# A table-lookup MLP on one core: first-layer sums split into two banks by chunk parity, with the next half transposed ahead of a half's product

## The reference

```
emb = tables[t][cat[t]]                      # 26 tables, 512 x 128 each
linear = sum over t of emb[t] + relu(numerical @ w_wide + b_wide)
x = relu(concat(numerical, emb[0], ..., emb[25]) @ W1 + b1)     # 3341 -> 256
x = relu(x @ W2 + b2)                                           # 256 -> 128
y = sigmoid(x @ W3 + b3 + linear)                               # 512 x 128
```

## Time and profile before

| | |
|---|---|
| median of 3 runs | 248.84 us (247.8 to 249.22) |
| the profiled execution's own time | 247.35 us |
| its span, first to last instruction | 245.5 us |
| PE busy | 110.2 us (45%) |
| POOL busy | 95.0 us (39%) |
| DVE busy | 37.7 us (15%) |
| ACT busy | 21.0 us (9%) |
| mean granted PE clock | 0.791 |

### The profile page before, as it was taken

One profiled execution on the slowest core, in us unless ns is written; L12 is line 12 of the kernel. 1 busy time (PEld: TensorE's weight loads), 2 busy tenths in 40 slices (PEclk: granted clock), 3 DMA queues, 4 the chain that ended last, 5 costly groups with the idle time before them and its releaser, 6 DMA issues.

```text
span 245.5 us, 2014 instructions
## 1 busy us (share of the span) xinstructions
PE 110.2 (45%) x398; PEld 67.5 (28%) x398; DVE 37.7 (15%) x106; ACT 21.0 (9%) x45; POOL 95.0 (39%) x108
## 2 busy tenths in 40 slices
PE   2657004500700004500009059979799991007795
PEld 0143001300300001300004026545466660005594
DVE  2031001000100002000001023244244430001132
ACT  0100000000000000000000001011011120001242
POOL 5777777777777777777750000000000000000000
PEclk9999999955695555875555759999999997555999
DMA  6994315444443353433231012131000000000001
GB/s 189 297 234 100 58 50 89 62 51 50 103 56 51 58 46 95 57 50 54 54 54 43 0 47 72 62 87 52 8 3 4 4 1 3 1 2 0 0 13 32
DMA packets 11163, 14.05 MB, mean 57 GB/s; under 512 B 3196, under 2 KB 8031, under 8 KB 11151
## 3 DMA queue, kind: packets, MB, share of 16 engines
q0 software_dynamic: 3168, 6.49, 17.7%
q10 hardware_dynamic: 3359, 3.63, 5.1%
q1 hardware_dynamic: 4624, 3.80, 5.1%
HBM read 13.65 MB, written 0.26 MB: 57 GB/s over the span
## 4 chain that ended last, share of the span: by engine, by line
SPq 54%; issue 35%; PE 8%; DMA 1%; ACT 1%; DVE 1%; ACTq 0%; DVEq 0%
SPq L229 48%; SPq L224 6%; PE first_layer L335 2%; PE first_layer L378 2%; PE mlp L401 1%; DMA first_cat<-in_r_cat_features 1%; ACT emb_t L559 1%; PE turn L320 1%; DMA emb<-in_L_rec_tables 0%; PE total L409 0%; PE turn L369 0%; PE total L395 0%; PE first_layer L351 0%; PE total L390 0%; ACT late_t L572 0%
## 5 line engine op out<-in xcount | busy, mean ns | idle before, releaser
L335 PE MATMUL first_layer<-emb_t,w 128*128 128x512 f32 (+3 forms) x104 | 58.2, 692 | 104.2 <-issue 90.3
L270 POOL DMA_INDIRECT emb<-in_L_rec_tables,row_idx x98 | 92.5, 944 | 30.0 <-issue 29.5
L335 PEld LDWEIGHTS first_layer<-emb_t,w 128*128 128x128 f32 x104 | 21.9, 231 | 124.4 <-issue 106.2
L500 DVE TENSOR_TENSOR emb_sum<-turn,emb_sum 128x512 f32<-128x512 f32 (+3 forms) x25 | 16.0, 638 | 182.0 <-issue 106.4
L559 ACT COPY emb_t<-turn 128x512 f32<-128x512 f32 (+3 forms) x26 | 14.1, 544 | 207.5 <-PE turn L320 75.8
L320 PE MATMUL turn<-ident,emb 128*128 128x128 f32 x94 | 17.6, 314 | 20.7 <-DMA emb<-in_L_rec_tables 18.1
L344 PE MATMUL total<-hot,block_rows 128*128 128x256 f32 (+1 forms) x98 | 25.0, 386 | 0.0
L320 PEld LDWEIGHTS turn<-ident,emb 128*128 128x128 f32 x94 | 14.3, 166 | 36.1 <-issue 35.8
L344 PEld LDWEIGHTS total<-hot,block_rows 128*128 128x128 f32 (+1 forms) x98 | 17.8, 199 | 1.6
L486 DVE TENSOR_SCALAR hot<-pick_row,row_no 128x256 f32<-128x256 f32 x49 | 14.8, 352 | 0.0
L378 PE MATMUL first_layer<-late_t,w 128*128 128x128 f32 x32 | 5.4, 291 | 0.6 <-ACT late_t L572 0.4
(11 more groups left out here) (51 smaller groups left out, 28.9 us busy)
## 6 DMA issues: line engine op xcount, KB each, us to landing
emb<-in_L_rec_tables SPq DMA_DIRECT2D x256, 0.5 KB
block_rows<-in_L_rec_tables ACTq DMA_DIRECT2D x12, 256.0 KB, 2.8
w<-in_L_rec_W SPq DMA_DIRECT2D x2, 1152.0 KB
emb<-in_L_rec_tables ACTq DMA_DIRECT2D x128, 0.5 KB
emb<-in_L_rec_tables,row_idx POOLq DMA_INDIRECT x98
w<-in_L_rec_W SPq DMA_DIRECT2D x1, 768.0 KB, 5.2
w<-in_L_rec_W SPq DMA_DIRECT2D x1, 256.0 KB
out<-y SPq DMA_DIRECT2D x4, 64.0 KB, 1.6
```

Source lines behind the costliest of these rows:

```text
L270: nc.gpsimd.indirect_dma_start(emb[:, t, c, :], None, rows, bass.IndirectOffsetOnAxis(ap=index, axis=0)).then_inc(landed, 16)
L335: mm = nc.tensor.matmul(first_layer[k][:, cols], w1[:, t, chunk(k)], emb_t[:, i % SLOTS, cols], start=False, stop=False, skip_group_check= ...
L500: nc.vector.tensor_tensor(emb_sum[:, cols], turn[i % 2][:, cols], emb_sum[:, cols], ALU.add).then_inc(added, 1)
```

## The change

The 512 columns of the first layer are held as two halves: half 0 is chunks 0 and 2, half 1 is chunks 1 and 3. Each has a bank of 256 used columns for each half of the hidden units (four banks in place of two, and the two banks `mlp` are gone; the second layer writes into free columns of the banks `first_layer[0][q]`). PARTS is now 47 half tables in place of 26 mostly whole ones, so every part has two tiles. Tile (0, 2) moves into an earlier part together with (0, 0), and (0, 1) and (0, 3) make part 44. Behind it stand only the two halves of table 25.

PE now transposes part i+1 before it multiplies part i. `emb_t` has 6 slots of 256 columns in place of 4 of 512. ACT issues 4 row fetches after each copy in place of 8. The late tables are 23 and 24. Their transposed tiles are added into `emb_sum` by DVE (`add_tile`), so that one product (`begin_total`) brings the sum into `total`. The picked tiles are chunks 1 and 3 of table 12, and their product stands right after part 40. The order of the tail is written anew. SP's program, the number of gathers (99), of row fetches (384), of pieces (13) and of one-hot blocks (49) stay as they are.

```diff
-LATE = 2
-HALVED = 2
-SLOTS = 4
+LATE_TABLES = (23, 24)
+SLOTS = 6
-ROWS_A_STEP = 8
-PICK_TABLE = 22
-PICK_FROM = 2
+ROWS_A_STEP = 4
+PICK_TABLE = 12
+PICK_HALF = 1
...
+    OTHERS = [t for t in range(1, T) if t not in LATE_TABLES]
+    PARTS = [(t, q) for t in OTHERS[:-4] for q in range(2)] + [(0, 0)]
+    PARTS += [(t, q) for t in OTHERS[-4:-1] for q in range(2)] + [(0, 1)]
+    PARTS += [(t, q) for t in OTHERS[-1:] for q in range(2)]
+    PARTS.remove((PICK_TABLE, PICK_HALF))
+    PICK_PARTS = (2, LAST - 8)
+    PICK_END = LAST - 7
+    def tiles(i):
+        t, q = PARTS[i]
+        return [(t, q + 2 * j) for j in range(HALF)]
...
+        def late_turn(n):
+            return turn[(LAST + n) % 2][:, 0:P]
+        def first_half(k, q):
+            return first_layer[k][q][:, 0:HW]
+        def first_chunk(k, c):
+            return first_layer[k][c % 2][:, chunk(c // 2)]
+        def second_chunk(c):
+            return first_layer[0][c % 2][:, HW + c // 2 * P:HW + (c // 2 + 1) * P]
...
+            turn_part(0)
             for i in range(LAST):
-                turn_part(i)
+                if i + 1 < LAST:
+                    turn_part(i + 1)
                 for j in blocks(i):
                     pick_block(j)
-                sum_part(i)
+                if i + 1 < LAST:
+                    sum_part(i)
                 if i == PICK_END:
                     sum_picked()
...
             def sum_tile(n):
                 c, g = divmod(n, LATE)
                 pe.wait_ge(late_copied, n + 1)
-                for k, (done, ready) in enumerate([(h1_low_done, h1_low_ready), (h1_high_done, h1_high_ready)]):
-                    if c >= 1 and g == 0:
-                        pe.wait_ge(ready, c)
+                if c >= 2:
+                    pe.wait_ge(h2_ready, c - 1)
...
             for c in range(CH):
                 n = c * LATE
                 turn_tile(n)
-                if c >= 1:
-                    add_late(c - 1)
+                if c == 0:
+                    sum_part(LAST - 1)
+                else:
+                    sum_tile(n - 1)
+                    begin_total(c - 1)
+                if c >= 2:
+                    layer3(c - 2)
+                turn_tile(n + 1)
+                sum_tile(n)
+                if 1 <= c < CH - 1:
                     layer2(c - 1)
-                sum_tile(n)
-                turn_tile(n + 1)
-                begin_total(c)
-                if c >= 1:
-                    layer3(c - 1)
-                sum_tile(n + 1)
-            add_late(CH - 1)
+            sum_tile(TILES - 1)
+            layer2(CH - 2)
             layer2(CH - 1)
+            layer3(CH - 2)
+            begin_total(CH - 1)
             layer3(CH - 1)
...
+            def add_tile(n):
+                c, g = divmod(n, LATE)
+                dve.wait_ge(late_copied, n + 1)
+                if n == 0:
+                    dve.wait_ge(added, LAST)
+                else:
+                    dve.wait_ge(late_added, n)
+                nc.vector.tensor_tensor(sum_chunk(c), late_turn(n), sum_chunk(c), ALU.add).then_inc(late_added, 1)
             for c in range(CH):
-                sum_late(c)
-                relu_h1_high(c)
-                relu_h2(c)
+                add_tile(c * LATE)
+                if c >= 1:
+                    relu_h1_high(c - 1)
+                add_tile(c * LATE + 1)
+                if 1 <= c < CH - 1:
+                    relu_h2(c - 1)
+            relu_h1_high(CH - 1)
+            relu_h2(CH - 2)
+            relu_h2(CH - 1)
...
             for c in range(CH):
                 copy_tile(c * LATE)
+                if c >= 1:
+                    relu_h1_low(c - 1)
+                if c >= 2:
+                    squash(c - 2)
                 copy_tile(c * LATE + 1)
-                if c >= 1:
-                    squash(c - 1)
-                relu_h1_low(c)
+            relu_h1_low(CH - 1)
+            squash(CH - 2)
             squash(CH - 1)
```

More of the change, by code:

```diff
@@ L66, in rows_apart @@
         return (t, c) in BY_SYNC + BY_SCALAR
-    BODY_TILES = [(0, 0)] + [(t, c) for t, lo, hi in PARTS for c in range(lo, hi) if (t, c) != (0, 0) and not rows_apart(t, c)]
+    BODY_TILES = [(0, 0)] + [tile for i in range(LAST) for tile in tiles(i) if tile != (0, 0) and not rows_apart(*tile)]
     def part_of(t, c):
-        return next(i for i, (u, lo, hi) in enumerate(PARTS) if u == t and lo <= c < hi)
+        return PARTS.index((t, c % 2))
     def by_pool(i):
-        t, lo, hi = PARTS[i]
-        return sum(not rows_apart(t, c) for c in range(lo, hi))
+        return sum(not rows_apart(t, c) for t, c in tiles(i))
     rows = tables.rearrange("t v d -> (t v) d")
@@ L282, in _ @@
                 c, g = divmod(n, LATE)
-                gather(BODY + g, c, column(BODY + g, c), late_gathered[n])
+                gather(LATE_TABLES[g], c, column(LATE_TABLES[g], c), late_gathered[n])
         @block.tensor
@@ L299, in _ @@
             pe.wait_ge(w1_num_loaded, 16)
-            for k in range(KH):
-                nc.tensor.matmul(first_layer[k][:, :], w1_num[:, chunk(k)], num_t[0:NUM, :], start=True, stop=True)
+            for q in range(2):
+                cols = num_t[0:NUM, :].rearrange("n (j q p) -> n q j p", j=HALF, q=2)[:, q, :, :]
+                for k in range(KH):
+                    nc.tensor.matmul(first_half(k, q), w1_num[:, chunk(k)], cols, start=True, stop=True)
             pe.wait_ge(small_loaded, 16 * SMALL)
@@ L316, in turn_part @@
                     pe.wait_ge(added, i - 1)
-                for c in range(lo, hi):
+                for j, (t, c) in enumerate(tiles(i)):
                     if (t, c) in fetched:
                         pe.wait_ge(fetched[t, c], 16 * P)
-                    mm = nc.tensor.transpose(turn[i % 2][:, chunk(c)], emb[:, t, c, :], ident[:, :])
+                    mm = nc.tensor.transpose(turn[i % 2][:, chunk(j)], emb[:, t, c, :], ident[:, :])
                 mm.then_inc(turned, 1)
@@ L383, in begin_total @@
             def begin_total(c):
-                if c == 0:
-                    pe.wait_ge(added, LAST)
-                    pe.wait_ge(pick_added, 1)
+                pe.wait_ge(late_added, (c + 1) * LATE)
                 if c >= 2:
                     pe.wait_ge(y_ready, c - 1)
[L390 to L396, removed]
+                nc.tensor.matmul(total_of(c), sum_chunk(c), ident[:, :], start=True, stop=False, skip_group_check=True)
             def layer2(c):
@@ L544, in _ @@
             act.dma_start(w2[:, :, :], W2.rearrange("(k p) n -> p k n", p=P)).then_inc(small_loaded, 16)
-            act.dma_start(pick_cat[:, :], cat[PICK_TABLE, PC:B].partition_broadcast(P)).then_inc(pick_cat_loaded, 16)
+            for j in range(HALF):
+                c = PICK_HALF + 2 * j
+                act.dma_start(pick_cat[:, chunk(j)], cat[PICK_TABLE, chunk(c)].partition_broadcast(P)
+                              ).then_inc(pick_cat_loaded, 16)
             act.wait_ge(ident_steps, 2)
@@ L553, in _ @@
             regs = []
-            for i, (_, lo, hi) in enumerate(PARTS):
-                cols = slice(lo * P, hi * P)
+            for i in range(LAST):
                 act.wait_ge(turned, i + 1)
@@ L571, in copy_tile @@
                 act.wait_ge(late_turned, n + 1)
-                nc.scalar.copy(late_t[:, n, :], turn[n % 2][:, 0:P]).then_inc(late_copied, 1)
+                nc.scalar.copy(late_t[:, n, :], late_turn(n)).then_inc(late_copied, 1)
             def relu_h1_low(c):
                 act.wait_ge(h1_low_done, c + 1)
-                nc.scalar.activation(h1[:, 0, chunk(c)], first_layer[0][:, chunk(c)], ACT.Relu,
+                nc.scalar.activation(h1[:, 0, chunk(c)], first_chunk(0, c), ACT.Relu,
                                      bias=b1_col[:, 0:1]).then_inc(h1_low_ready, 1)
```

91 lines of the change are left out of this document (39 added, 52 removed).

## The result

The changed kernel takes 241.48 us (median of 4 runs, 240.63 to 241.65) against 248.47 us before; the ratio is 0.971, 95% interval 0.9683 to 0.9737. Forecast were 243.5 us and a range of 237.5 to 250.

What follows compares the result with a forecast made beforehand. SP's row fetches were taken to bound the kernel. Gains of 4.1 us behind the landing and 1.3 us in the tail took 247.35 to 241.95 us; with the median 1.5 us above, 243.5 us was forecast, range 237.5 to 250.

Steps and rivals of the forecast that it cites:

- What bounds the kernel: Whole kernel: SP's row fetches end at 221.7 us, plus 21.5 us of work behind, plus 2.3 us for sigmoid and store.
- SP's chain at zero: SP's row fetches: program and 99 gathers unchanged, so cost zero, with 4 us either way as uncertainty.
- first two rivals: SP's slow stretch gets shorter or quicker, 231 to 240 us (chance 0.14), or longer, 245 to 254 us (chance 0.19).
- The rule of the Trainium skill: Slow stretch: SP's slowness would hang on how many trace records the core makes; 231 to 240 or 245 to 254 us.
- The body under cover: Half parts ahead of the landing: end at 206 to 216 us, 6 to 16 us of cover, cost zero.
- Behind the landing: From tile (0, 3)'s landing to the second late tile's transpose: 6.3 us, no gaps for copies, 4.1 us gained.
- Tail: Work from the second late tile's transpose on: 9.1 us against 10.43 before, 1.3 us gained.
- Sum: Whole kernel: 5.4 us less, 241.95 us for the profiled execution; median 1.5 us above that, 243.5 us.

## Why the prediction was right, and where it was off

**What bounds the kernel.** Right: SP's last row sets the start of the end. With SP's second tile given to POOL, and product 43 ahead of part 44, the time falls by 15.6 us on the same chip. How much of that is the product's place isn't separated; behind a landing it was worth 0.9 to 1.9 us.

**SP's chain at zero.** Right to 0.8 us: the last row landed at 222.6 and not 221.8 us, which is no more than it varies between executions. Neither of the first two rivals came about: the stretch ended at 143.03 against 143.01 us, with 8 table pieces in it by then and not 6, and half as many rows to a copy. The slowness is there in one lot and not in another, and ACT is held up beside POOL's gathers also without any row fetch. The rule of the Trainium skill weighed there ("NOTIFIC — the notification-queue block", section 7.1: inside, the block that takes down the records holds its producers back and loses none) is neither shown nor excluded by that, since no run here shows the block.

**The body under cover.** Right: 8 half parts by 143 us (6 to 9 were said), the end at 206.8 us (206 to 216), 15.8 us of cover (6 to 16). That transposing ahead would save as much as 12.6 us here was not said; it costs and gains nothing until the cover goes.

**Behind the landing.** The order and the missing gaps were right. The term was 6.3 us to the second late tile and measured 5.9. The clock was back within the second product and not behind it. When it returns is not the kernel's alone: the same kernel on another chip needed 6.65 us for this. So that the term came out within 0.4 us is in part luck.

**Tail.** This term was mis-sized by the most: 9.1 us forecast, 8.34 measured. I counted the second layer at 0.55 to 0.61 us; 0.55 is its distance to the next group in the earlier trace rows (236.40 to 236.95), and in the new order that distance is 0.45 (230.47 to 230.92 in the changed kernel). That is 0.1 to 0.15 us for each chunk. I had rounded the other steps up by about 0.1 each, and the sum takes the last product to its end while the 10.43 us beside it goes to its start, which is 0.2 more. The two passes saved for each chunk are 0.89 us of the 2.09 gained; the other 1.20 are there also in the run that sums the late tiles as before (9.23 against 10.43), so they come from the rest of the new tail. Which of its waits gives how much isn't shown.

**Sum.** The profiled execution was forecast at 241.95 us and took 241.46. It is this close because misses offset each other: 0.8 us lost at the landing, 0.4 and 0.8 gained behind it. The median was forecast 1.5 us above it, since the kernel before had been so in three runs; after the change the two agree (241.46 and 241.48). That offset lies within what executions differ by and was not to be added, and it is most of the 2.0 us between forecast and median. The gain in medians, 7.0 us, is 1.2 above that in spans for the same reason.

**What stays open.** What the slow stretch is, and why it ends so long after the last gather. It was seen in lots where the kernel before takes 248 us, holds SP, ACT and with it PE, leaves POOL's cadence alone, and ends 16.0 to 16.8 us after POOL's last gather starts. No two lots of the experiments had the same chip, so whether it belongs to the chip or to something else that differs between lots isn't told. And the changed kernel itself was not timed on a chip without it: its variants with one more gather gained 2.6 to 2.7% there. That this is the shorter tail, behind the last gather, is likely and not shown.

## What to carry to other kernels

Find the transfer whose landing starts the end of the kernel, and price an edit by what it leaves behind that landing; 12.6 us saved ahead of it went into the wait for it here, and a product more behind it costs 0.9 to 1.9 us. Look also at what a transpose made ahead takes with it: everything issued between it and the product it passes waits for the same landing. The larger prize was the transfer itself: giving half of SP's rows to POOL, with one product moved, was worth 15.6 us on one kind of chip. On the other it costs about one gather (1.2 us), as an estimate from the 2.4 us that two gathers cost there. So such a choice wants timing on more than one chip.

## What the runs showed of the hardware

- The same program takes 248 us on some chips and 142.5 us on others (of the six lots timed, four were of the first kind and two of the second). On the first kind each instruction of SP takes 0.70 us beside POOL's gathers and a row 2.8 us; on the second a row takes 0.40 us all the time. POOL issues a gather each 1.25 us on both.
- On the first kind ACT's copies come once in 22 us in that stretch, with four rows to issue between them or none. The stretch ends 16.0 to 16.8 us after POOL's last gather starts: 142.6 to 143.2 us with 99 gathers, 144.4 with 100, 146.7 with 102.
- PE's clock can fall behind a landing: after 2.3 us of waiting a product took 1.13 us (granted clock 1.00) and the one 1.9 us later 2.08 (0.53).
- The same order of work behind the same kind of wait (15.7 to 15.9 us) took 5.89, 6.65 and 6.90 us to the same transpose in three executions: the second product after the landing took 1.60 us in the first of them and 1.91 in the other two, as long as the first product.
